# x1 of blocks 2 to 6 turned by a DMA transpose of 16-bit planes, with new due steps, in a recurrent sandwich layer

## What is computed

```python
def layernorm(x): return (x - mean(x)) / sqrt(var(x) + 1e-5)

def recurrent(x):
    u = x @ W_in.T + b_in                       # 512 -> 1024
    s = 0
    for t in range(1024):                       # one step after another
        s = tanh(u[:, t] + s * gamma + beta)
        states[:, t] = s
    return states @ W_out.T + b_out             # 1024 -> 512

def ffn(x):                                     # weights rounded to e4m3
    gate = silu((x @ q(gate_w)) * gate_scale)   # 512 -> 1536
    up = (x @ q(up_w)) * up_scale
    return ((gate * up) @ q(down_w)) * down_scale

x1 = x + layernorm(recurrent(layernorm(x)))
out = x1 + layernorm(ffn(layernorm(x1)))
```

## Time and profile before

| | us |
|---|---|
| median of 3 runs | 557.66 (557.09 to 560.22) |
| profiled execution, first to last instruction (span) | 556.6 |
| TensorE matmul busy | 540.2 (97%) |
| TensorE weight load busy | 457.6 (82%) |
| VectorE busy | 444.8 (80%) |
| ScalarE busy | 374.8 (67%) |
| GpSimd busy | 228.0 (41%) |
| mean granted TensorE clock | 0.994 of 2.4 GHz |

### The profile page before, as it was taken

How to read it: one execution, slowest core, us unless ns; L and a number is a source line. 1 busy time by engine, 2 the same in 40 slices (tenths; PEclk the granted TensorE clock), 3 DMA queues, 4 the chain that set the end, 5 groups by cost and what they waited for, 6 DMA issues and landing times.

```text
span 556.6 us, 11947 instructions
## 1 busy us (share of the span) xinstructions
PE 540.2 (97%) x2958; PEld 457.6 (82%) x2958; DVE 444.8 (80%) x2608; ACT 374.8 (67%) x2317; POOL 228.0 (41%) x372
## 2 busy tenths in 40 slices
PE   8998989999899999999999999999999999999995
PEld 5846769888688888898889888987888887899994
DVE  3699999978797998878987899778988898874414
ACT  3687687864578777877678667876787777762332
POOL 1222446475446541652338222562341321633532
PEclk9999989999999999999999999999999999999998
DMA  8789398991104200120003000300002000200011
GB/s 275 248 268 250 83 226 154 258 158 40 46 13 153 60 1 1 56 80 2 1 2 114 20 1 2 109 6 2 1 2 77 1 2 2 76 2 1 1 39 38
DMA packets 25334, 39.92 MB, mean 72 GB/s; under 512 B 3761, under 2 KB 8497, under 8 KB 25265
## 3 DMA queue, kind: packets, MB, share of 16 engines
q1 hardware_dynamic: 19904, 30.24, 16.7%
q0 software_dynamic: 4608, 8.39, 8.9%
q10 hardware_dynamic: 752, 0.54, 0.3%
HBM read 26.57 MB, written 4.20 MB: 55 GB/s over the span
## 4 chain that ended last, share of the span: by engine, by line
PE 67%; DVE 4%; ACT 1%; POOL 1%; issue 0%; POOLq 0%; DVEq 0%; ACTq 0%
PE gate_up L1131 25%; PE wide L1087 15%; PE wide L1161 13%; PE wide L1056 12%; DVE recur L1231 1%; PE wide L1107 1%; DVE recur_second L1231 1%; ACT pairs L1556 1%; DVE z L1377 0%; DVE stats_z L1245 0%; POOL z L1744 0%; DVE fused L1364 0%; ACT gated L1591 0%; DVE x_lo L1346 0%; POOL norms L1669 0%
## 5 line engine op out<-in xcount | busy, mean ns | idle before, releaser
L1556 ACT ACTIVATE pairs<-recur 128x8 f32<-128x8 f32 x768 | 137.3, 179 | 90.3 <-DVE recur L1231 90.2
L1231 DVE TENSOR_TENSOR_SCAN recur<-recur,pairs 128x16 f32<-128x16 f32 x768 | 151.0, 197 | 48.1 <-ACT pairs L1556 45.8
L1556 ACT ACTIVATE pairs<-recur_second 128x8 f32<-128x8 f32 x768 | 136.8, 178 | 0.0
L1231 DVE TENSOR_TENSOR_SCAN recur_second<-recur_second,pairs 128x16 f32<-128x16 f32 x768 | 133.2, 173 | 0.0
L1754 POOL TENSOR_TENSOR fused_lo<-fused,fused_hi 128x256 fp32r<-128x256 f32 x95 | 70.4, 743 | 127.9 <-ACT fused_hi L1609 126.0
L1087 PE MATMUL wide<-w_out_sb,pairs 128*128 128x512 f32 (+1 forms) x272 | 112.5, 563 | 0.2 <-ACT pairs L1565 0.2
L1056 PE MATMUL wide<-x_norm_t,w_in_sb 128*128 128x256 f32 x448 | 102.7, 382 | 3.7 <-ACT x_norm_t L1507 3.7
L1056 PEld LDWEIGHTS wide<-x_norm_t,w_in_sb 128*128 128x128 f32 x448 | 84.6, 191 | 16.3 <-ACT x_norm_t L1507 4.3
L1087 PEld LDWEIGHTS wide<-w_out_sb,pairs 128*128 128x128 f32 x272 | 75.5, 298 | 25.9 <-ACT pairs L1565 0.7
L1161 PE MATMUL wide<-down_q,fused_hi 128*128 128x512 f32 x192 | 81.7, 425 | 1.9 <-POOL fused_lo L1754 1.9
L1591 ACT ACTIVATE gated<-gate_up,gate_scale_cols 128x128 f32<-128x128 f32 (+1 forms) x169 | 63.4, 378 | 27.0 <-PE gate_up L1131 26.8
(11 more groups left out here) (135 smaller groups left out, 777.2 us busy)
## 6 DMA issues: line engine op xcount, KB each, us to landing
x_res<-x SPq DMA_DIRECT2D x16, 256.0 KB, 3.3
x_in<-x SPq DMA_DIRECT2D x14, 256.0 KB, 4.6
out<-z SPq DMA_DIRECT2D x14, 256.0 KB, 2.5
x_norm_t<-x_t SPq DMA_DIRECT2D x5, 512.0 KB, 4.9
raw_own<-rounders POOLq DMA_DIRECT2D x9, 256.0 KB, 5.2
w_in_sb<-w_in_t SPq DMA_DIRECT2D x4, 512.0 KB, 7.0
w_out_sb<-w_out_t SPq DMA_DIRECT2D x8, 256.0 KB, 5.4
raw_own<-down_w SPq DMA_DIRECT2D x8, 256.0 KB, 4.7
```

The costliest lines, as they stand in the source:

```text
L1231: eng.tensor_tensor_scan(preact_of[b].rearrange("p c k -> p (c k)"), factors_of[b].rearrange("p c k -> p (c k)"), pairs[:, t % RING, colum ...
L1556: ins = eng.activation(pairs[:, t % RING + 1, columns, 0], preact_of[b][:, :, 1], ACT.Tanh)
```

## The change

For blocks 2 to 6 (`by_planes`) the eight TensorE transposes of x1_norm are gone. In their place, for each half: GpSimd copies x1_norm as 16-bit halves into two planes of 128x512 (`x1_planes`, in the memory of `powers`); SP issues one DMA transpose of the 128x1024 16-bit elements, that is eight 128x128 blocks, into `x1_turned`; GpSimd copies the two turned planes back into 32-bit words (`x1_words`, one tile for each half, in the memory of `raw_own`). ScalarE's x1_hi and VectorE's x1_lo read x1_words in SBUF. A copy into planes waits for the DMA before it, a DMA for the copy back before it, and a copy back of block 3 on for the x1_lo of the same half one block earlier. Blocks 0, 1 and 7 still use TensorE; block 6 was on bank wide[b] and is so no more, and gate_up and down of the blocks from 2 on no longer wait for a shared bank ahead of x1. The lists of due steps are all new, for every block.

```diff
-CHUNKS_FROM = [132.7, 268.4, 380.8, 538.3, 671.1, 894.2, 988.8, 1038.6]
-CHUNKS_PER_BLOCK = [10, 13.5, 13, 10.5, 10, 6, 8.5, 11]
+CHUNKS_FROM = [231.2, 93.2, 291.4, 704.5, 111.4, 909.7, 861.6, 576.3]
+CHUNKS_PER_BLOCK = [31.0, 34.5, 20.0, 28.5, 24.0, 24.0, 26.0, 48.5]
+INPUTS_FROM = [-930.2, -83.2, 317.3, 175.2, 208.8, 496.2, 1744.8, 949.2]
...
+TURNED_X1_FROM = 2
+PLANE_STEPS, TURN_LANDS = 3.0, 8.0
...
     def transpose_x1(n, b, after, k):
-        tensor(("t2", n, b), TRANSPOSE_STEPS, [(v, 0.2) for v in rows("r", "r_norm", n, b)] + after, ROWS_TURNED[batch * n + b])
+        if by_planes(n):
+            again = by_planes(n - 1)
+            planes = [(v, 0.2) for v in rows("r", "r_norm", n, b)]
+            if again or b > 0:
+                planes += [(("x1_words", *((n, b - 1) if b > 0 else (n - 1, batch - 1))), 0.0)]
+            side("gpsimd", ("x1_planes", n, b), planes, k, PLANE_STEPS)
+            t.add("sync", ("x1_turn", n, b), ISSUE_STEPS, [(("x1_planes", n, b), 0.2)], 0.0)
+            words = [(("x1_turn", n, b), TURN_LANDS)]
...
+            side("gpsimd", ("x1_words", n, b), words, k, PLANE_STEPS)
+            turned = ("x1_words", n, b)
...
+            def turn_x1():
+                for n in filter(by_planes, range(NB)):
+                    for b in range(batch):
+                        yield at["x1_turn", n, b]
+                        eng.wait_ge(s_x1_planes, plane_turns(n, b))
+                        if plane_turns(n, b) > 1:
+                            eng.wait_ge(s_x1_words, plane_turns(n, b) - 1)
+                        eng.dma_start_transpose(out=x1_turned.rearrange("p (g t) -> p g t", t=P), in_=x1_planes
+                                                ).then_inc(s_x1_turned, 16)
...
             def transpose_x1():
                 for n in range(NB):
+                    if by_planes(n):
+                        continue
...
-                        elif n < LAST - 1:
+                        elif n < LAST:
                             eng.wait_ge(s_z_scaled, rows_through("z", n - 1, b))
...
+                        x1_t = x1_words[b] if by_planes(n) else x1_bank(n, b)
                         ins = eng.tensor_tensor(x1_lo[:, ks, b * P:(b + 1) * P],
-                                                x1_bank(n, b)[:, row_slice("low", n, b, h)].rearrange(
+                                                x1_t[:, row_slice("low", n, b, h)].rearrange(
...
+            def split_x1():
...
+                        eng.tensor_copy(x1_planes.rearrange("p (v d) -> p v d", v=2),
+                                        x1_norm[:, b, :].bitcast(U16).rearrange("p (d v) -> p v d", v=2)).then_inc(s_x1_planes, 1)
+
+            def join_x1():
...
+                        eng.wait_ge(s_x1_turned, 16 * plane_turns(n, b))
+                        if by_planes(n - 1):
+                            eng.wait_ge(s_x1_lo, batch * (n - 1) + b + 1)
+                        eng.tensor_copy(x1_words[b].bitcast(U16).rearrange("p (c v) -> p c v", v=2),
+                                        x1_turned.rearrange("p (v c) -> p c v", v=2)).then_inc(s_x1_words, 1)
```

More of the change, by code:

```diff
@@ L165 @@
 TWO_CHAINS_FROM = 2
+LAST_BLOCK = 7
 LAST_CHUNK = 11
@@ L274, in project_u @@
                 after += [(v, 0.2) for v in rows("y", "y_copy", n - 2, m)]
+                if n == 2:
+                    after += [(("u_copy", 1, m + 2, q), 0.2) for q in range(4)]
             if n == 1 and m < 2:
@@ L297, in project_y @@
                 else:
-                    after += [(v, 0.2) for v in rows("low", "x1_low", n - 1, b)]
+                    after += [(v, 0.2) for v in rows("y", "y_copy", n - 1, b)]
                 if (n, b) == (0, 1):
@@ L357, in down @@
             after += [(("gate_up", p, KI - 1), 0.0)]
-        if i == 0 and p < LAST - 1:
+        if i == 0 and p < TURNED_X1_FROM:
             after += [(v, 0.2) for b in range(batch) for v in rows("low", "x1_low", p, b)]
@@ L634, in recurrent_sandwich_kernel @@
         powers = sb("powers", [P, dim])
+        x1_planes, x1_turned = powers[:, :].bitcast(U16), raw_own[:, batch, :].bitcast(U16)
+        x1_words = [raw_own[:, b, :] for b in range(batch)]
         signed_ident = fused_hi[:, 0, :].rearrange("p (s c) -> p s c", s=2)
@@ L830, in x1_bank, with turned_on_tensor, plane_turns, wait_x1_read @@
         def x1_bank(n, b):
-            return wide[b] if n >= LAST - 1 else wide[2 + b]
+            return wide[b] if n == LAST else wide[2 + b]
+        def turned_on_tensor(n, b):
+            return batch * sum(not by_planes(m) for m in range(n)) + b + 1
+        def plane_turns(n, b):
+            return batch * sum(by_planes(m) for m in range(n)) + b + 1
+        def wait_x1_read(eng, n, b):
+            if by_planes(n):
+                eng.wait_ge(s_x1_planes, plane_turns(n, b))
+            else:
+                eng.wait_ge(s_t2, turned_on_tensor(n, b))
+        def last_raw_use(r):
+            return max(i for i in range(NP) if raw_of[i] == r)
         def x_bank(b):
@@ L1047, in project_u @@
                             eng.wait_ge(s_y_copied, rows_through("y", n - 2, bank))
+                            if n == 2:
+                                eng.wait_ge(s_u_rows, 3 + bank)
                         if n == 1 and m == 2:
```

64 lines of the change are left out of this document (48 added, 16 removed).

## The result

| | before | after |
|---|---|---|
| median of 4 runs each, same chip, us | 558.12 (557.09 to 560.22) | 563.64 (563.28 to 564.62) |
| ratio | | 1.0098 (1.0079 to 1.0117) |
| profiled execution: time and span, us | span 556.6 | 564.62, span 562.8 |

The change costs 5.5 us, twice what a measurement of this kernel can tell from no change. 557.3 was forecast, as "no change that counts"; the range, up to 567, holds the result.

The account below looks back on a forecast made before the run. TensorE's total work and the recurrence were taken as joint limits. The wait at block 6 made the span 558.8; less 2.5 of shorter recurrence, 556.3; plus 1.0 from profiled span to median, 557.3 us, range 551.5 to 567.

Parts of the forecast that it names:

- no change that counts: Whole kernel: TensorE work saved and the wait before block 6 cancel, 557.3 us; the likeliest case, chance 0.37.
- What comes back: Recurrence: lighter TensorE and fewer VectorE waits for y shorten it by 2.5 us, of a possible 13.
- Rival 3: VectorE beside GpSimd: x1_low, x_res and x_norm instructions collide with GpSimd work, 7 us lost, 564 us; chance 0.11.
- Hardly vary beside 145 us of GpSimd work: VectorE: argument against collisions, from x_res taking 324 to 487 ns, median 327, in the kernel before.
- I price that difference at nothing to a gain of 0.05 us each: ScalarE's x1 copies and VectorE's subtraction: reading SBUF instead of PSUM costs nothing or gains 0.05 us each.
- Block 6: TensorE without cover there: waits until 467.3, does y in 7.0 us, starts gate_up at 474.3; span 558.8 us.
- The path of x1: From x1_norm to turned x1: copy 1.4, DMA 3.7, copy back 1.4, handovers 0.4, together 6.9 us (4.3 to 10.5).
- Rival 2: Blocks 2 to 5: the DMA transpose lands late, at 6.9 us, stalling each block by 3.2; 570 or 564 us; chance 0.17.
- Rival 1: Whole kernel faster: recurrence shorter by 4 us or more, block 6's wait shrinks, TensorE's sum bounds at 553.3 us; chance 0.35.
- I see no row in which the transposes themselves delay a scan: Recurrence: argument against the faster case, that the TensorE transposes do not hold up the scans.
- with the recurrence as it is: Tail: if the recurrence stays unchanged, only 1.7 us of TensorE backlog comes off, giving 554.9 us.
- TensorE's busy time near 536: TensorE over the whole kernel: a sign of being right, busy time falling from 540.2 to near 536 us.

Follow-up runs that it names:

- e1: The changed kernel with x1_lo of blocks 2 to 6 written as zeros by VectorE, so it reads no inputs: 560.90 us.
- e12: The changed kernel with semaphore waits on GpSimd alone, so that what follows x1_low in the timetable waits for it: 560.91 us.
- e2: The changed kernel with block 6 turned on TensorE again, on its old bank, and planes in blocks 2 to 5: 560.42 us.
- e13: The changed kernel with block 6 back on TensorE and semaphore waits on GpSimd behind x1_low, all work kept: 559.31 us, ratio 1.0035 to before.
- e6: The kernel before with 30 of the 40 transposes of blocks 2 to 6 left out, all orders and waits the same: 555.91 us.
- e9: The changed kernel with x1_lo of blocks 2 to 6 as SCALAR_TENSOR_TENSOR, the form of x_res, on VectorE: 562.74 us.
- e5: The changed kernel with block 6 on TensorE and x1_lo of the plane blocks written as zeros: 559.38 us, ratio 1.0012 to before.
- e14: The changed kernel with planes in blocks 3 to 5 alone, blocks 2 and 6 on TensorE, and semaphore waits on GpSimd: 558.50 us.
- e7: The changed kernel with x1_lo of blocks 2 to 6 subtracted by GpSimd instead of VectorE, nothing left out: 559.96 us.
- e8: The changed kernel with block 6 on TensorE and x1_lo of blocks 2 to 5 subtracted by GpSimd: 559.56 us.

## Why the prediction was wrong, point by point

- **The step that failed is "What comes back": 2.5 us of shorter recurrence.** It became 5.0 us longer (356.5 against 351.5). What it counted on did come: VectorE's waits for y in this stage went from 2.7 to 0.3 us. But the six collisions (e1 and e12: 2.9 and 3.2 us) and the path at block 6 (in e2 the recurrence is 3.3 shorter, 1.5 of these in its last 64 scans) outweigh it. Each of these sizes can hold up to 0.9 us of the clock, since the kernel after has more time at half rate in its profile. With both cured (e13) 352.4 is left, 0.9 above before. The sum had a term for waits that would go and none for those that would come. e6 puts the gain without any of the costs at 2.2 us of the whole time for 30 of the 40 transposes.
- **Rival 3 was the right mechanism for half of the loss, at 0.11, argued against with the wrong row.** "Hardly vary beside 145 us of GpSimd work" is true of rows 12 and says nothing: between 144 and 500 us none of these instructions began inside GpSimd's work of more than one element per partition. The shares of the two engines are no measure of how they meet; the timeline at the 54 places would have been. Its price was not far off: six instructions of twenty and 4.8 us, where ten of a hundred and 7 us were taken; but they are all x1_low's, and x_res and x_norm, which were counted in, are kept clear by the plan. That its 564 meets the measured 563.64 is luck: the collisions alone are worth 2.7 us (e1), and the path at block 6 makes up most of the rest (e2, 3.2). The Trainium skill, GPSIMD Engine Reference, "Key points", states this contention for two SBUF inputs; the trace of after agrees (0.68 to 1.56 us where 0.41 is the undisturbed time), and that of before shows no case of it. "I price that difference at nothing to a gain of 0.05 us each" is the same error on x1_lo.
- **Block 6: right in kind, 3.6 us short.** Forecast: wait until 467.3, y, gate_up at 474.3. Measured: the scan steps for y are there at 469.9 (2.8 late, from the longer recurrence), the down products held by fused_lo end at 471.7 (1.6 more), y takes 6.3 instead of 7.0: 477.9. The 6.3 are not a faster y: only twelve of its sixteen matmuls stand there, the other four come at 482.1, and the first ones start 0.85 us apart, at half rate, where e12 has 0.43 and starts the same twelve within 4.7 us instead of 6.25. So 1.5 us of the wait for gate_up is the clock's, a term that the sum did not have. The remaining TensorE work was forecast as 77.7 and took 78.0, these four matmuls among it. Without "what comes back" the sum stood at 558.8, and these 3.6 us and 0.4 more are the 4.0 to the measured span of 562.8.
- **The path of x1: right by two errors.** 6.9 us was forecast, 7.0 it took (464.6 to 471.6), but of other parts: copies of 1.04 and 1.15 us instead of 1.4, a landing of 3.1 instead of 3.7, and some 1.6 us between the landing (465.72 + 3.1) and the copy back at 470.48, in which GpSimd had fused_lo and x_res in line. 1024 elements of 16 bits cost neither what 512 of 32 bits do (0.69) nor twice that.
- **Rival 2 did not happen.** The transposes landed after 3.1 us, 4.1 at most, and GpSimd waited 6.9 us for them in all, in four waits. Of the two figures of the Trainium skill weighed in the prediction, the trace fits that of DMA: Bandwidth & Descriptors, "Latency and other measured facts" (1 us of transfer within the 3.1); it does not fit 1309 ns a block, of the Trainium skill, VectorE: DVE Perf Modes, "The three transpose paths", which as an estimate would be 10.5 us for the eight blocks of one transfer.
- **Rival 1 asked for too much**, but its link was real. e6 shows two thirds of such work coming off where nothing else changes, 2.0 of the 2.2 us through the recurrence. "I see no row in which the transposes themselves delay a scan" was the wrong conclusion from the rows, and the smaller of the prediction's two bounds, "with the recurrence as it is", had a condition that did not hold: in e6 it did not stay as it is.
- **TensorE's busy time near 536** was wrong by 3 us for this execution (539.1) and right for e9 (536.1), which has one stretch of 6.8 us at half rate less. The prediction gave holes their length alone.
- Outside the span lie 1.8 us (564.62 and 562.8), where 1.0 was taken; the other runs do not depend on it.

What stays open: 0.9 to 1.8 us between e5, e13 and the kernel before; the interval of e5 includes no difference, that of e13 does not. Why e1 and e2 do not add fully is open too. Whether another fitting of the due steps to e14 would turn its 5.0 us of idle time into a gain was not tried.

## What to carry to other kernels

Before an instruction gets a second SBUF input on VectorE, look in the timeline at what GpSimd does there, and at who starts first; a median and a maximum of other instructions tell nothing unless some of them began inside GpSimd's work. Where a plan keeps two engines apart by time alone, its margin has to be larger than its error (here GpSimd, 0.06 to 0.44 us ahead, cost VectorE up to 1.15 us at a time); semaphore waits on the engine that has slack gave 2.7 us back, 1.4 by the ratios. And work taken off the busiest engine is worth only what its successor can start earlier: put the latency of the new path beside the cover at the end of the pipeline first, since block 6, the last to go by planes, had hardly any.

## What the runs showed of the hardware

- A VectorE instruction with two SBUF inputs (128x256, 0.41 us alone) that began while a GpSimd instruction of 512 or 1024 elements per partition was running ended 0.27 to 0.29 us after that one, six of six in the kernel after (0.68 to 1.56 us), in both forms tried. One that began inside a GpSimd instruction of a single element took 0.40. With one PSUM input, begun inside GpSimd work of 256 or 512 elements, it took 0.40 to 0.41 (164.50, 413.27, 465.10 and 515.24 us before, 521.41 after).
- In the other order GpSimd lost little: fused_lo begun 0.21 to 0.24 us behind an x_res started and ran as always (0.08 us after its input, 0.74 long); z scaled from 0.06 us behind an x1_lo took 0.98 instead of 0.77.
- A DMA transpose of 128 x 1024 elements of 16 bits, SBUF to SBUF, landed 3.1 us after its issue, the median of ten, 4.1 the longest.
- A hole of 3.1 to 3.2 us in TensorE's work at the same place was met by 6.8 us at 1.2 GHz in the kernel after, 3.4 in e1, e5, e7, e8, e12 and e13, and none in e2 and e9.
- The spread between runs of one kernel goes with the granted clock in many sets: in e6, twelve runs between 554.8 us at a mean of 0.998 and 559.9 at 0.991, some 0.5 to 0.7 us for each 0.001, which is what a clock lower by that share would cost over the whole span (556 x 0.001). In the sets of the kernel before it is looser (558.31 us at 0.998 and 557.48 at 0.994 beside e14). When two kernels differ by less than 1%, look at the clocks too.
